# First block of head pair 0 (heads 0 and 1) projected row tile by row tile from turn seven on, in five banks

## What is computed

```python
x = x + _layernorm(_L0_attn_ref(_layernorm(x), Wq, Wk, Wv, Wo, bo))
x = x + _layernorm(_L0_ffn_ref(_layernorm(x), w1, b1, w2, b2))
# attention: x of 4 x 4096 x 1024, 16 heads of 64
q, k, v = (heads(Wq), heads(Wk), heads(Wv))
scores = einsum('bhqd,bhkd->bhqk', q, k) - slopes * dist   # causal
ctx = einsum('bhqk,bhkd->bhqd', softmax(scores / 8), v)
return ctx @ Wo + bo
```

## Time and profile before

| what | us |
|---|---|
| median of 3 runs | 1247.45 (1246.63 to 1248.32) |
| the profiled execution | 1246.88 |
| its slowest core, span from first to last instruction | 1245.3 (core 2) |
| the other cores' spans | 1239.6 to 1245.2 |
| TensorE busy on core 2 | 1163.5 |
| ScalarE busy on core 2 | 967.7 |
| VectorE busy on core 2 | 749.0 |

### The profile page before, as it was taken

The page is one execution under the profiler, slowest core; times in us unless marked ns, Lnnn a source line. Parts: engine busy times, 40 slices in busy tenths (PEclk is TensorE's granted clock), DMA queues, the critical chain, the costliest instruction groups (busy, mean ns, idle before and its releaser), DMA issues.

```text
span 1245.3 us, 27151 instructions; the slowest of 8 cores (1239.6 to 1245.3 us)
## 1 busy us (share of the span) xinstructions
PE 1163.5 (93%) x11328; PEld 643.8 (52%) x11328; DVE 749.0 (60%) x1607; ACT 967.7 (78%) x1202; POOL 179.1 (14%) x357
## 2 busy tenths in 40 slices
PE   3889989999999999999987999878999999999997
PEld 2565656656566565666654444433444444444443
DVE  7876443332434333243431789996888888888842
ACT  3449999999999999999998478886666677776710
POOL 4520010010100000000010343430111111111110
PEclk9899999999999999999998999989999999999999
DMA  9953533343533312111139765546333333333211
GB/s 259 262 155 58 98 72 59 57 86 61 92 57 67 67 30 54 25 36 23 32 63 177 219 194 153 163 117 152 105 108 110 110 116 122 127 110 109 70 68 68
DMA packets 62870, 128.00 MB, mean 103 GB/s; under 512 B 9238, under 2 KB 26134, under 8 KB 62108
## 3 DMA queue, kind: packets, MB, share of 16 engines
q1 hardware_dynamic: 53900, 101.10, 27.5%
q0 software_dynamic: 8848, 25.17, 13.1%
HBM read 117.84 MB, written 25.17 MB: 115 GB/s over the span
## 4 chain that ended last, share of the span: by engine, by line
PE 74%; DVE 12%; ACT 7%; DMA 4%; POOL 1%; issue 1%; SPq 0%; DVEq 0%; POOLq 0%; ACTq 0%
PE pW L897 17%; PE pF L824 14%; PE pjb L309 12%; PE S L402 9%; PE acc L455 9%; PE pjb L341 8%; ACT P L418 6%; DMA xst<-x_full 2%; PE pja L309 2%; DVE x L700 1%; DVE bst L228 1%; PE pW L673 1%; DVE bst L229 1%; DMA w1s<-w1bf 1%; DVE g L868 1%; DVE g L862 1%
## 5 line engine op out<-in xcount | busy, mean ns | idle before, releaser
L418 ACT ACTIVATE P<-S,biasT 128x1024 bf16<-128x1024 f32 (+1 forms) x576 | 563.0, 1083 | 21.2 <-PE S L402 19.5
L824 PE MATMUL pF<-xl2T,w1s 128*128 128x512 bf16 x1024 | 260.6, 384 | 14.4 <-ACT cu L839 11.2
L897 PE MATMUL pW<-w2s,hq 128*128 128x512 bf16 x1024 | 256.5, 380 | 0.0
L455 PEld LDWEIGHTS acc<-V,P 128*128 128x128 bf16 x4352 | 162.5, 97 | 53.0 <-DVE ctx L473 10.9
L402 PE MATMUL S<-Q,K 64*128 64x512 bf16 (+3 forms) x1280 | 174.9, 350 | 14.6 <-ACT P L418 12.8
L455 PE MATMUL acc<-V,P 128*128 128x66 bf16 x4352 | 180.0, 193 | 3.7 <-DVE ctx L473 2.0
L839 ACT ACTIVATE cu<-pF,b1s 128x512 int32<-128x512 f32 x128 | 87.9, 687 | 111.8 <-PE pF L824 110.7
L824 PEld LDWEIGHTS pF<-xl2T,w1s 128*128 128x128 bf16 x1024 | 100.1, 99 | 136.0 <-ACT cu L839 13.1
L309 PE MATMUL pjb<-xlT,W 128*128 128x512 bf16 x648 | 167.0, 381 | 2.1 <-DVE kst L319 0.8
L897 PEld LDWEIGHTS pW<-w2s,hq 128*128 128x128 bf16 x1024 | 100.4, 98 | 121.5 <-issue 1.1
L319 DVE CAST kst<-pjb 128x512 bf16<-128x512 f32 x81 | 56.0, 692 | 132.5 <-PE pjb L309 128.7
(11 more groups left out here) (78 smaller groups left out, 1110.0 us busy)
## 6 DMA issues: line engine op xcount, KB each, us to landing
w1s<-w1bf SPq DMA_DIRECT2D x128, 256.0 KB, 2.8
xst<-x_full SPq DMA_DIRECT2D x32, 512.0 KB, 10.8
K<-kst SPq DMA_DIRECT2D x128, 64.0 KB, 2.0
Q<-kst SPq DMA_DIRECT2D x128, 64.0 KB, 2.3
w1bf<-w POOLq DMA_DIRECT2D x32, 256.0 KB, 3.9
w2s<-w POOLq DMA_DIRECT2D x8, 1024.0 KB, 22.0
x<-x_full SPq DMA_DIRECT2D x16, 512.0 KB, 5.0
x2scr<-x SPq DMA_DIRECT2D x16, 512.0 KB, 3.5
```

What stands on the lines that cost most here:

```text
L418: t = put("scalar", lambda io: io.activation(out=P3[:, :, c0:512], in_=S[s][:].rearrange("p (o c) -> p o c", o=2)[:, :, c0:512], func=AF.E ...
L455: io.matmul(acc[:, q * 66:(q + 1) * 66], P[p][:, at:at + 128], zv[:, o, j, hh, :], start=st, stop=sp, skip_group_check=True),
L824: t = put("tensor", lambda io, c=c: io.matmul(pF[b][:], w1s[n % 4][:, c * 128:(c + 1) * 128], xl2T3[g][:, c, :], start=(c == 0), stop=(c = ...
L897: put("tensor", lambda io, ft=ft, hf=hf: io.matmul(pO[b][:, hf * 512:(hf + 1) * 512], slot_of(g, ft, tl), w2s[:, ft * 1024 + hf * 512:ft * ...
```

## The change

Five banks `pja` instead of three, and three banks `pT` instead of four, in the first stage (eight banks instead of seven).

Block 0 of head pair 0 is no longer worked unit by unit but row tile by row tile: its five units are open at once, one bank each, and a piece is now the eight matmuls of 128 columns for one row tile, for K and Q as well. From turn 7 on, each turn takes five such pieces, those of one own row tile and of one of the other core's (the list `early`): tiles 0 and 1 in turn 7, 2 and 3 in turn 8, 4 and 5 in turn 9, 6 and 7 in turn 10. In turn 8 the constants of V are filled. From turn 11 on `pieces(4, ...)` goes on as before, with the other units. A K or Q unit of every other block is still eight matmuls of 512 columns.

A V matmul group waits for its own row tile alone, where it waited for the fourth of its block.

```diff
--- before.py
+++ after.py
@@ -175,8 +175,8 @@
     with stk:
         ps = lambda s, nm_, cols, ty: s.enter_context(nc.psum_tensor(nm_, [128, cols], ty))
         st_a = contextlib.ExitStack()
-        pj_a = [ps(st_a, f"pja{i}", 512, F32) for i in range(3)]
-        pT = [ps(st_a, f"pT{i}", 1024, BF16) for i in range(4)]
+        pj_a = [ps(st_a, f"pja{i}", 512, F32) for i in range(5)]
+        pT = [ps(st_a, f"pT{i}", 1024, BF16) for i in range(3)]
         st_a.close()
         st_b = contextlib.ExitStack()
         pj_b = ps(st_b, "pjb", 512, F32)
@@ -250,7 +250,7 @@
 
         xlT3 = xlT[:].rearrange("p (c n) -> p c n", c=8)
         t_xT = {}
-        xfree, xlfree, pTfree = [None] * NX, [None] * 4, [None] * 4
+        xfree, xlfree, pTfree = [None] * NX, [None] * 4, [None] * 3
 
         def ln_load(t):
             return dma("sync", xst[t % NX][:], x_d[t * 128:(t + 1) * 128, :], f"x{t % NX}",
@@ -269,19 +269,19 @@
             tm = None
             for c in range(8):
                 tm = put("tensor", lambda io, c=c: io.transpose(
-                    pT[t % 4][:, c * 128:(c + 1) * 128], xl[t % 4][:, c * 128:(c + 1) * 128], ident[:]),
-                    after=[tn, pTfree[t % 4], t_id] if c == 0 else (), inc=(c == 7))
+                    pT[t % 3][:, c * 128:(c + 1) * 128], xl[t % 4][:, c * 128:(c + 1) * 128], ident[:]),
+                    after=[tn, pTfree[t % 3], t_id] if c == 0 else (), inc=(c == 7))
             xlfree[t % 4] = tm
             col = (t % 2) * MYN + (t // 2) * 128
             te = put("scalar", lambda io: io.copy(
-                out=xlT3[:, :, col:col + 128], in_=pT[t % 4][:].rearrange("p (c n) -> p c n", c=8)),
+                out=xlT3[:, :, col:col + 128], in_=pT[t % 3][:].rearrange("p (c n) -> p c n", c=8)),
                 after=[tm], inc=True)
-            pTfree[t % 4] = te
+            pTfree[t % 3] = te
             t_xT[t] = te
 
 
         pjn = {"i": 0}
-        pjs = {"banks": pj_a, "free": [None] * 3, "ev": "scalar"}
+        pjs = {"banks": pj_a, "free": [None] * 5, "ev": "scalar"}
         ksn = {"i": 0}
         evict_later = []
         kstfree = [None] * 4
@@ -304,13 +304,19 @@
                 w = 0 if kind == "q" else 1
                 col = blk * 512 + (MYN if kind == "ko" else 0)
                 t = None
-                last = 2 * (blk * 4 + 3) + (1 if kind == "ko" else 0)
-                for c in range(8):
-                    t = put("tensor", lambda io, c=c: io.matmul(
-                        pj[b][:], Wb[pb][w][:, c * 128:(c + 1) * 128], xlT3[:, c, col:col + 512],
-                        start=(c == 0), stop=(c == 7)),
-                        after=[pjfree[b], t_w[hp], t_xT[last]] if c == 0 else (), inc=(c == 7))
-                    if c % 2 == 1 and c < 7:
+                o = 1 if kind == "ko" else 0
+                if hp == 0 and blk == 0:
+
+                    todo = [(c, i, i + 1) for i in range(4) for c in range(8)]
+                else:
+                    todo = [(c, 0, 4) for c in range(8)]
+                for c, i0, i1 in todo:
+                    t = put("tensor", lambda io, c=c, i0=i0, i1=i1: io.matmul(
+                        pj[b][:, i0 * 128:i1 * 128], Wb[pb][w][:, c * 128:(c + 1) * 128],
+                        xlT3[:, c, col + i0 * 128:col + i1 * 128], start=(c == 0), stop=(c == 7)),
+                        after=[pjfree[b], t_w[hp], t_xT[2 * (blk * 4 + i1 - 1) + o]] if c == 0 else (),
+                        inc=(c == 7 and i1 == 4))
+                    if (c, i1) != (7, 4) and (c == 7 or i1 - i0 == 4 and c % 2 == 1):
                         yield 1
                 if pjs["ev"] == "scalar":
                     t = put("scalar", lambda io: io.copy(out=kst[s][:], in_=pj[b][:]),
@@ -341,7 +347,7 @@
                         t = put("tensor", lambda io, c=c, i=i, col=col: io.matmul(
                             pj[b][:, i * 128:(i + 1) * 128], xlT3[:, c, col:col + 128],
                             Wb[pb][2][:, c * 128:(c + 1) * 128], start=(c == 0), stop=(c == 7)),
-                            after=[pjfree[b], t_w[hp], t_xT[2 * (blk * 4 + 3) + o]] if c == 0 else (),
+                            after=[pjfree[b], t_w[hp], t_xT[2 * (blk * 4 + i) + o]] if c == 0 else (),
                             inc=(c == 7 and i == 3))
                     if i < 3:
                         yield 1
@@ -478,6 +484,10 @@
 
         units = {hp: proj_units(hp) for hp in range(HP)}
         gen, pend = None, None
+        first = [units[0].pop(0)[2] for _ in range(6)]
+        z0 = first.pop(3)
+        early = [(2 * i + o, u) for i in range(4) for o, us in ((0, (0, 2, 3)), (1, (1, 4)))
+                 for u in (first[n] for n in us)]
 
         def pieces(n, blocks):
 
@@ -503,8 +513,15 @@
             if t in (2, 10):
                 t_w[t // 10] = load_w(t // 10)
             pend = (t, k, t_r)
-            if t > 8:
-                pieces(4, (t - 1) // 8)
+            if t > 6:
+                if t == 8:
+                    next(z0)
+                n = 5 if early else 4
+                while n and early and early[0][0] < t - 1:
+                    next(early.pop(0)[1])
+                    n -= 1
+                if not early:
+                    pieces(n, (t - 1) // 8)
         ln_b(*pend)
         if gen:
             for _ in gen:
```

## The result

The changed kernel is slower, by more than forecast. Its runs took 1259.21, 1259.71 and 1260.5 us, beside 1246.63 to 1252.51 for the kernel before; the ratio is 1.0097 [1.0067, 1.0128]. (Each batch also holds runs in which the cores of one die or of both ran at a lower clock and took some per cent longer; all comparisons here leave them out.) I had said 1251, at most 1257. The profiled execution took 1259.21 us. The slowest core is now 4, with 7 close behind, where it was core 2; in the other two runs it is core 7 and core 0, so which core is last is partly chance.

A forecast was written before the change was run, and what follows sets the result against it. TensorE, 74% of the chain, was taken to bound the kernel. On core 5, +7.3 us first stage and -3.2 attention gave 1249.3; adding 1.6 and 0.3 gave 1251.2, stated as 1251 us. Forecast band 1250 to 1254, range 1246 to 1257.

The forecast's parts named there:

- The start of the projections: First stage, turn 7: its forty matmuls wait for pair 0's weights until 29.9 us, holding row tile 7's transposes; ends 33.5.
- the slow rate: First projections after TensorE's idle time: the first 2.8 us of matmuls run slowly, half of it lost, +1.4 us.
- VectorE's hold: First stage, turn 10: V evictions stand ahead of tile 10's normalisation on VectorE; its transposes start at 43.2 us.
- The gaps in the V turns: First stage after turn 10: TensorE idles some 1.7 us before transposes in each of six V turns.
- The second weights: First stage, weights of pair 1: land 3.4 us sooner, at 43.4 us, so no wait and the clock stays.
- rival (a): First stage: second weights land as now and the clock falls, +3.1 and +3.0 us, total about 1256; chance 0.15.
- What comes back: Attention: two V units fewer, 3.6 us of TensorE, at 88% of the chain give -3.2 us; bounds 2.5 and 3.6.
- The slowest core: Whole kernel: core 5 ends last, stage +7.3 and attention -3.2, so +4.1 us, 1249.3.
- my correction by 0.4: End of first stage: the same reckoning for the kernel before came 0.4 us late, so 100.5 was taken as 100.1.
- (b): Whole kernel: no measurable difference, by V gaps under 1.7 us or 5 us lost and 3.6 back; 1248.5 to 1249.5; chance 0.27.
- (c): First stage after turn 10: VectorE's own work sets the pace, making the kernel faster, 1244.9 us; chance 0.08.
- (d): First stage: the early start is none, as the weights are not there; part of the forecast, no chance of its own.

The follow-up runs named there:

- e2: Changed kernel with V's evictions queued on VectorE behind the next row tile's normalisation: 1251.2 us, ratio 1.0033 to the kernel before.
- e8: Changed kernel with only the weights of pair 1 issued earlier, in turn 7 instead of 10: 1256.96 us, one run.
- e5: Kernel before with V units of head pairs 2 to 7 multiplying seven of eight slices: 1238.05 us, one run.
- e9: Kernel before with the two V units of pair 1's block 1 multiplying one slice of eight: 1247.68 us.
- e1: Changed kernel with pair 0's weights issued in turn 0 (not 2), pair 1's in turn 5 (not 10): 1254.73 us, ratio 1.0061 to the kernel before.
- e3: Changed kernel with the row-wise pieces starting in turn 9 instead of 7: 1250.96 us, ratio 1.0034 to the kernel before.
- e12: Changed kernel, from turn 7 as written, with V's evictions behind the normalised tile and pair 1's weights issued in turn 7: 1248.32 us, one run.
- e11: Changed kernel from turn 9 on, with V's evictions behind the normalised tile and pair 1's weights issued in turn 7: 1243.48 us, one run.
- e10: Kernel before with V's evictions behind the normalised tile and pair 1's weights issued in turn 7: 1243.78 us, ratio 0.9971.

## Why the prediction was right in direction and short in size

**The start of the projections** held. I had "until 29.5 to 31 us"; the cores wait until 29.1 to 30.1, 0.7 us sooner than my two cores' sums had it on the mean. Turn 7 was to end at 33.5, and T(7) stands at 33.82 on core 4. The step that was small here is the slow rate: I took the 2.8 us of the kernel before, +1.4. On core 4 the groups of eight take 1.06 us for 0.61 until 34.7. That is 5 us at the slow rate, and from turn 7's start to T(10) 14.6 us (29.57 to 44.13) where my sum has 13.3 (29.9 to 43.2): 1.3 more. On the mean of the cores it is 14.25, 0.95 more. That T(10) still comes close to its forecast is in part luck: the earlier start pays for most of the longer slow rate.

**VectorE's hold** held in its mechanism and was a little longer: 6 to 8 us of waiting forecast, 8.79 on core 4; T(10) forecast at 43.2, at 44.00 on core 2 and 44.13 on core 4. **The gaps in the V turns** held: six of 1.60 and 1.66 against 1.7. e2 shows what both together are worth, 7.65 us, net of a longer second wait.

**The second weights** are the step that failed. I wrote "with two tiles fewer in the way the weights land 3.4 us sooner" and took no wait. The second issue came when I had it, at 32.3 to 33.4 us, and on core 4 the last of the three lands 12.9 us after its issue, no sooner than in the kernel before (12.0); on all cores it is 12.0 to 13.5 us, and 11.5 to 12.3 before. There was less beside them (core 4's DMAs moved 3.98 MB from 30 to 47 us, 4.86 before), and it made them no quicker. At the end that isn't for want of bandwidth: the stretches above have 148 and 107 GB/s from 42 to 46 us, where the kernel before moved 271 and 277. The wait of 1.0 to 3.3 us and the clock behind it were my rival (a), with a chance of 0.15. I had priced it at +3.1 and +3.0 us on top. With the wait partly covered by VectorE's hold it is 3.7 on the mean of the cores, from T(10) to T(16) against e8, and 3.05 by the first score matmul, since e8 loses some again behind the gap ahead of T(16). The Trainium skill (DMA: Bandwidth & Descriptors, Issuing engines are not separate DMA queues) says that transfers of several engines interleave on the same 16 DMA engines. That doesn't contradict it, but it doesn't carry what I drew from it: that a load with less company lands sooner.

**What comes back** is the other step that failed. I priced the spared matmuls at TensorE's share of the whole attention's chain, 88%, and for matmuls spared evenly that holds: e5 measured 87%. But what is left of pair 1 stands in pair 0's steps alone, and behind it comes a stretch in which ScalarE binds by itself (theory D). So 3.6 us taken from TensorE gave 1.04, not 3.2 (e9: 0.82 for 3.1). My lower bound of 2.5 had no row of those steps behind it. A stretch of the trace of before shows it at once: 12.10 of 12.10 us of ScalarE from 157.9 to 170.

**The slowest core.** I forecast core 5, by +4.1. Cores 4 and 7 came out slowest in the profiled execution, and 7 and 0 in the two other runs. Core 4's first stage was among the short ones before, 92.42 us, and it lost 15.5: besides the second wait, its clock fell once more after a V gap, at 62.40, worth 1.6 us (from 62.40 to 66.21 are 3.81 us, where a tile's transposes and a K unit otherwise take 2.2), and on no other core. I had named that as a thing that no row shows, and left it out; the change makes it possible, since the kernel before has no such gaps, and e1 and e8 show it on three and four cores.

In numbers: I had forecast +5.2 to +7.3 for the stage and -3.2 for the attention, in sum +2.0 to +4.1. Measured on the mean of the cores are +12.26 and -1.04, +11.2. Between the middle of the forecast, +3.0, and +11.2 lie 8.2 us. Of these 0.9 are no error of mechanism: my sums were for cores 2 and 5, whose stage ended later than the mean in the kernel before (94.1 against 93.25). The rest, on the mean of the cores: 3.7 are the second weights and their clock, 2.2 the attention, 0.3 the later T(10) (43.8 for 43.5), and 0.2 the fallen clock behind a gap (core 4's 1.6 over eight cores). Another 0.4 lie in the turns from T(10) to T(31), 55.7 us where nothing disturbs them for my 55.3, and 0.5 in the step from T(31) to the first score matmul, 2.1 us for the 1.6 that my correction by 0.4 had left. So the two failed steps make up 5.9 of the 8.2.

The rivals: (b), no measurable difference, asked for gaps well below 1.7, or for a stage 5 us longer with 3.6 to come back, and fell with the gaps, the +12.26 and the 1.04. (c), VectorE's own pace, fell with the 8.79 us that it waits. (d), that the early start is none, was in the forecast, and e3 and e12 against e11 confirm and price it.

## What to carry to other kernels

An eviction that waits for a late matmul should not stand in its engine's queue ahead of work that the matmul engine needs next: two swapped lines were worth 3.8 us in the kernel before and 7.65 in the changed one. Starting work earlier in program order is no gain where its operands are not there, and costs whatever stands behind it in the queue; the load has to come sooner first, and where loads bind as a whole (e1, e10) that delays another. And before counting spared work at the whole stage's rate, look which steps it is spared in, and how full the second engine is in just those.

## What I had not expected of the hardware

- **The weights landed no sooner on emptying queues.** The three matrices (256 KB each on the page) took 8.6, 10.2 and 12.9 us on core 4. The DMA engines are busy for over nine tenths of the time until about 42 us, and for ever less after that. What GpSimd's queue moved from 33 to 47 us (q0 is GpSimd's queue: packets, MB, share of 16 engines) and in the end of that stretch:

```profile
q0 software_dynamic: 432, 0.79, 36.1%
```

```profile
DMA  7929133598822100599682200110000000033997
...
q0 software_dynamic: 12, 0.02, 3.9%
```

  The second fence is 44 to 46.7 us. Only 12 of the 432 packets are left at 44 us, the last of them is seen before 45.6, and TensorE's first matmul with these weights starts at 46.74. The 16 DMA engines are mostly idle meanwhile (the digits are their busy share in tenths, in 40 slices). Which engine or which request holds the tail, and what lies between the last packet and the matmul, the runs don't tell; it stays open.
- **A gap of 1.66 us was followed by a lower clock on some cores.** In three kernels it is the gap ahead of T(16) behind which the clock falls: on one core in the changed kernel (4, at 62.40 us), on three in e1 and on four in e8, at a cost of 1.6 to 1.7 us each. The other gaps of 1.60 in these kernels are not followed by one. What makes the difference stays open. The Trainium skill (TensorE: Matmul & The Clock Gate, Loop structure matters more than you think) ties a falling clock to long waits on DMA; here one fell behind a short wait for VectorE.
- **The half rate isn't always in the granted clock.** From the first transposes at 9.86 us to 34.67 us on core 4 groups of eight matmuls take 1.01 to 1.06 us for 0.61, and the granted clock reads 1.00; behind the second wait it reads 0.50. At the first projections of the kernel before the full rate was there after 2.8 us, here after 5.1. How long it lasts can't be taken over from another kernel.
